# Row maxima copied into every pair of score banks by ScalarE and spread over the partitions by DMA, in place of a fourth pair of score products

## The reference

```python
x = L0_attn_queries                       # (4, 1024, 256)
xn = _layernorm(x, axis=-1)
x = x + attention(xn, Wq, Wkv, Wout, bout) + fp4_ffn(xn, w_gate, w_up, w_down)
```

## Time and profile before

| what | value |
|---|---|
| time, 3 runs | median 1957.51 us (1953.85 to 1958.97) |
| profiled execution | 1953.43 us; its span 1951.6 us |
| mean granted TensorE clock in it | 0.987 |
| busy share of the span | PE 96%, PEld 59%, DVE 76%, ACT 42%, POOL 71% |
| steady attention steps | some 475 to 1765 us of the span |

### The profile page before, as it was taken

How to read it: one execution, slowest core, us unless ns; L and a number is a source line. 1 busy time by engine, 2 the same in 40 slices (tenths; PEclk the granted TensorE clock), 3 DMA queues, 4 the chain that set the end, 5 groups by cost and what they waited for, 6 DMA issues and landing times.

```text
span 1951.6 us, 29139 instructions
## 1 busy us (share of the span) xinstructions
PE 1870.8 (96%) x10916; PEld 1151.1 (59%) x10916; DVE 1480.8 (76%) x2032; ACT 822.5 (42%) x1078; POOL 1394.7 (71%) x688
## 2 busy tenths in 40 slices
PE   6989999859999999999999999999999999999989
PEld 4768899835555555555555555555555555555589
DVE  7969999887777777777777777777777777776254
ACT  4643333214444444444444444444444444444432
POOL 4764544408888888888888888888888888889900
PEclk9989999969999999999999999999999999999999
DMA  8550311110212132122123211212322112211474
GB/s 287 227 189 30 136 36 49 47 54 20 60 53 58 53 99 62 53 64 57 54 67 95 58 53 52 63 56 57 96 64 67 54 53 58 52 50 47 144 258 171
DMA packets 151165, 161.29 MB, mean 83 GB/s; under 512 B 43248, under 2 KB 107376, under 8 KB 150768
## 3 DMA queue, kind: packets, MB, share of 16 engines
q1 hardware_dynamic: 151024, 159.43, 25.9%
HBM read 100.14 MB, written 59.24 MB: 82 GB/s over the span
## 4 chain that ended last, share of the span: by engine, by line
PE 61%; DVE 21%; issue 6%; POOL 3%; DMA 1%; ACT 0%; SPq 0%; POOLq 0%; DVEq 0%; ACTq 0%
PE banks L1004 17%; PE banks L1024 12%; PE banks L947 10%; PE banks L981 8%; PE banks L1007 6%; PE banks L1033 3%; POOL acc L1201 3%; DVE half_max L1077 3%; PE banks L1514 2%; DVE q_lo L1122 2%; DVE k_lo L1122 2%; DVE h_scales L110 2%; DVE f_y L131 2%; DVE f_amax L109 1%; DVE f_y L134 1%
## 5 line engine op out<-in xcount | busy, mean ns | idle before, releaser
L1201 POOL TENSOR_TENSOR acc<-acc,prob 128x1024 f32<-128x1024 f32 x384 | 917.4, 2389 | 131.0 <-ACT prob L1240 102.3
L1077 DVE TENSOR_REDUCE half_max<-banks 128x2 f32<-128x1024 f32 x512 | 627.5, 1227 | 298.2 <-PE banks L981 298.2
L1240 ACT ACTIVATE prob<-banks 128x1024 f32<-128x1024 f32 x512 | 512.2, 1026 | 621.5 <-PE banks L1007 621.5
L1024 PE MATMUL banks<-prob,v 128*64 128x512 f32 x2048 | 495.7, 605 | 0.0
L1024 PEld LDWEIGHTS banks<-prob,v 128*64 128x64 f32 x2048 | 124.2, 136 | 240.1 <-issue 191.2
L1201 POOL TENSOR_TENSOR acc<-prob,prob 128x1024 f32<-128x1024 f32 x64 | 153.6, 2400 | 150.3 <-ACT prob L1240 150.3
L981 PE MATMUL banks<-k_hi,q_hi 64*128 64x512 f32 x1024 | 233.4, 452 | 12.5 <-DVE half_max L1077 10.9
L947 PE MATMUL banks<-xT,wqk 128*128 128x512 f32 x768 | 217.6, 420 | 3.5 <-DVE k_lo L1122 2.1
L981 PEld LDWEIGHTS banks<-k_hi,q_hi 64*128 64x128 f32 x1024 | 97.7, 187 | 187.6 <-issue 150.5
L1007 PE MATMUL banks<-max_rows,ones_r 64*128 64x512 f32 x1024 | 203.7, 392 | 0.0
L1004 PE MATMUL banks<-q_hi,k_hi 64*128 64x512 f32 x1024 | 203.7, 393 | 0.0
(11 more groups left out here) (121 smaller groups left out, 2192.9 us busy)
## 6 DMA issues: line engine op xcount, KB each, us to landing
v_scratch<-v_out SPq DMA_DIRECT2D x32, 512.0 KB, 2.6
wqk<-wp_scratch SPq DMA_DIRECT2D x32, 512.0 KB, 3.5
v<-v_scratch SPq DMA_DIRECT2D x32, 512.0 KB, 4.8
inv_rows<-inv_scratch SPq DMA_DIRECT2D x128, 128.0 KB, 3.3
o_scratch<-o_norm SPq DMA_DIRECT2D x64, 256.0 KB, 2.0
o_in<-o_scratch SPq DMA_DIRECT2D x8, 2048.0 KB, 11.3
xn_scratch<-p_xT SPq DMA_DIRECT2D x32, 256.0 KB, 2.9
xT<-xn_scratch SPq DMA_DIRECT2D x8, 1024.0 KB, 5.8
```

The lines of the kernel that those rows point to most:

```text
L1024: ins = nc.tensor.matmul(o_ps[head * DH:(head + 1) * DH, :], v[s % 2][:, kt, at:at + DH], prob[n % SLOTS][:, head, :], start=kt == 0, stop ...
L1077: nc.vector.tensor_reduce(half_max[:, half % 2, :, t % GRP, part], guess_bank(s, i), axis=AX.X, op=ALU.max, negate=True).then_inc(half_max ...
L1201: nc.gpsimd.tensor_tensor(acc[b][:, :, :], first, prob[n % SLOTS][:, :, :], ALU.add).then_inc(added, 1)
L1240: nc.scalar.activation(prob[n % SLOTS][:, :, :], s_ps[n % 2][:, :, :], ACT.Exp).then_inc(exp_done, 1)
```

## The change

The transposition, the multiplication by the pattern, and the fourth pair of each unit's products go. In their place

- `combine` writes only the 8 columns; SP stores them to DRAM (`store_max`, new L1340, elements of 4 B), and reads all 1024 numbers (512 queries, two heads) back into each of the 128 partitions (`spread_max`, new L1349) as `max_all`,
- ScalarE copies `max_all` into the pair of score banks ahead of each unit's products (`seed`, new L1216, Copy, 128 x 1024, 512 times),
- the remaining three pairs are added on top of it, with `start=False`, and wait for `seeded`.

`seed(n+2)` stands right behind `exponent(n)` in ScalarE's order. The waits of `scores` on `exp_done` and `rows_done` become one on `seeded`; `seed(n+2)` takes over the one on `exp_done`, here on an exponential of the same engine.

```diff
@@ scores
-            if kt == 0:
-                pe.wait_ge(rows_done, 2 * s + half + 1)
-            if n >= 2:
-
-                pe.wait_ge(exp_done, n - 1)
-            elif n == 1:
-                pe.wait_ge(kept["h_high"], TILES)
+            pe.wait_ge(seeded, n + 1)
...
-                    nc.tensor.matmul(s_ps[n % 2][:, head, :], left[rows, keys], right[rows, queries], start=k == 0, stop=False)
-            for head in range(2):
-                rows = slice(head * DH, (head + 1) * DH)
-                ins = nc.tensor.matmul(s_ps[n % 2][:, head, :], ones_r[rows, :], max_rows[half][rows, :], start=False, stop=True)
+                    ins = nc.tensor.matmul(s_ps[n % 2][:, head, :], left[rows, keys], right[rows, queries], start=False, stop=k == 2,
+                                           skip_group_check=True)
             ins.then_inc(scored, 1)
@@ scalar
+        def seed(n):
+
+            s, u = divmod(n, UNITS)
+            if u % QT == 0:
+                act.wait_ge(max_in[u // QT], 16 * (s + 1))
+            if n == 0:
+                act.wait_ge(lo_done, Q0 + 1)
+            elif n == 1:
+                act.wait_ge(half_maxed, UNITS)
+            else:
+
+                act.wait_ge(exp_done, n - 1)
+            nc.scalar.activation(s_ps[n % 2][:, :, :], max_all[u // QT][:, :, :], ACT.Copy).then_inc(seeded, 1)
...
                 if scoring(s):
                     exponent(s * UNITS + 2 * r)
+                    if s * UNITS + 2 * r + 2 < STEPS * UNITS:
+                        seed(s * UNITS + 2 * r + 2)
                 if r == 0 and scoring(s + 1) and s >= 0:
                     high(act, s + 1, Q1)
                 if r in (2, 4, 6) and scoring(s + 2):
                     high(act, s + 2, CHUNK_ROUND[r - 1])
                 if scoring(s):
                     exponent(s * UNITS + 2 * r + 1)
+                    if s * UNITS + 2 * r + 3 < STEPS * UNITS:
+                        seed(s * UNITS + 2 * r + 3)
@@ sync
+        def store_max(s, half):
+
+            if s:
+
+                sp.wait_ge(max_in[half], 16 * s)
+            sp.wait_ge(max_done, 2 * s + half + 1)
+            sp.dma_start(io["max_scratch"][half].rearrange("h t p -> p h t"), max_cols[half][:, :, :],
+                         allow_slow_non_contiguous=True).then_inc(max_stored[half], 16)
+
+        def spread_max(s, half):
+
+            sp.wait_ge(max_stored[half], 16 * (s + 1))
+            if s:
+
+                sp.wait_ge(scored, (s - 1) * UNITS + (half + 1) * QT)
+            sp.dma_start(max_all[half][:, :, :].rearrange("p h c -> p (h c)"),
+                         io["max_scratch"][half].rearrange("h t p -> (h t p)").partition_broadcast(P)).then_inc(max_in[half], 16)
...
+            if scoring(s):
+                store_max(s, 1)
             if scoring(s - 1):
                 spread_inverse(2 * (s - 1))
+            if scoring(s):
+                spread_max(s, 1)
...
                 store_o(2 * (s - 1))
+            if scoring(s + 1):
+                store_max(s + 1, 0)
+                spread_max(s + 1, 0)
             if scoring(s - 1):
                 spread_inverse(2 * (s - 1) + 1)
```

More of the change, by code:

```diff
@@ L822, in misc_table @@
                 job("sum", s, 0)
[L823 to L826, removed]
     return table
@@ L850, in attention_part @@
     shuffled = [first(f"shuffled{i}", [P, GCOL], F32) for i in range(2)]
-    own = small("own", [P, GRP], F32)
     ones = small("ones", [P, DH], F32)
-    ones_r = small("ones_r", [P, P], F32R)
     half_max = small("half_max", [P, 2, 2, GRP, 2], F32)
-    max_cols = [small(f"max_cols{i}", [P, P], F32) for i in range(2)]
-    max_rows = [small(f"max_rows{i}", [P, GCOL], F32R) for i in range(2)]
+    max_cols = [small(f"max_cols{i}", [P, 2, GRP], F32) for i in range(2)]
     compact = small("compact", [P, 2, 2, GRP], F32)
@@ L868, in attention_part @@
     o_norm = [late(f"o_norm{i}", [P, GCOL], F32) for i in range(2)]
+    max_all = [late(f"max_all{i}", [P, 2, GCOL], F32) for i in range(2)]
     bout = late("bout", [P, D], F32)
@@ L883, in attention_part @@
     res_stored, wp_stored, down_done = kept["res_stored"], kept["wp_stored"], kept["down_done"]
-    guessed, half_maxed, max_done, rows_done = sem("guessed"), sem("half_maxed"), sem("max_done"), sem("rows_done")
+    guessed, half_maxed, max_done, seeded = sem("guessed"), sem("half_maxed"), sem("max_done"), sem("seeded")
+    max_stored, max_in = [sem(f"max_stored{i}") for i in range(2)], [sem(f"max_in{i}") for i in range(2)]
     scored, exp_done, pv_done, added = kept["scored"], sem("exp_done"), kept["pv_done"], kept["added"]
@@ L929, in begin @@
             pe.wait_ge(lo_done, 4 * s + k + 1)
-        elif before == "turn":
-            pe.wait_ge(rows_done, 2 * s + k + 1)
         else:
@@ L1034, in column_sums @@
             ins.then_inc(misc_done, 1)
[L1036 to L1042, removed]
+        pe.wait_ge(cleared, 1)
         for s in range(-2, STEPS + 1):
@@ L1062, in tensor @@
                     column_sums(s, 0)
[L1063 to L1066, removed]
     def vector(dve):
@@ L1082, in combine @@
             dve.wait_ge(half_maxed, s * UNITS + (half + 1) * QT)
[L1083 to L1088, removed]
             if s:
[L1091 to L1094, removed]
+                dve.wait_ge(max_stored[half], 16 * s)
+            nc.vector.tensor_reduce(max_cols[half][:, :, :], half_max[:, half, :, :, :], axis=AX.X, op=ALU.min).then_inc(max_done, 1)
         def rotate(s, chunk):
@@ L1129, in invert @@
             nc.vector.reciprocal(inv_compact[:, b, :, :], compact[:, b, :, :]).then_inc(inv_done, 1)
-        dve.wait_ge(cleared, 4)
-        dve.wait_ge(tables_in, 32)
+        dve.wait_ge(tables_in, 16)
         rotate(0, K0)
@@ L1143, in vector @@
                     maximum(s + 1, 2 * r)
-                if r == 1 and scoring(s):
-                    spread_rows(s, 1)
-                if r == 5 and scoring(s + 1):
-                    spread_rows(s + 1, 0)
                 if r == 0 and scoring(s + 1) and s >= 0:
@@ L1270, in scalar @@
                     exponent(s * UNITS + 2 * r + 1)
+                    if s * UNITS + 2 * r + 3 < STEPS * UNITS:
+                        seed(s * UNITS + 2 * r + 3)
+                elif s == -1 and r == ROUNDS - 1:
+                    seed(0)
+                    seed(1)
                 if s == STEPS - 1 and r in (2, 3, 4, 5):
@@ L1400, in clear @@
     def clear(dve):
-        nc.vector.memset(max_cols[0][:, :], 0.0).then_inc(cleared, 1)
-        nc.vector.memset(max_cols[1][:, :], 0.0).then_inc(cleared, 1)
         nc.vector.memset(ones[:, :], 1.0).then_inc(cleared, 1)
-        nc.vector.memset(ones_r[:, :].bitcast(F32), 1.0).then_inc(cleared, 1)
     def first_loads(sp):
@@ L1412, in first_loads @@
         load_x(sp, 0, 1)
-        sp.dma_start(own[:, :], io["tables"][:, P + 2 * SEQ:]).then_inc(tables_in, 16)
         load_wqk(sp, 1)
@@ L1639, in shape_constants @@
             turn[head * DH + dim, 1] = sin[:, dim // 2] if dim % 2 == 0 else -sin[:, dim // 2]
-    own = (np.arange(P)[:, None] % DH == np.arange(GRP)[None, :]).astype(np.float32)
-    return np.concatenate([np.eye(P, dtype=np.float32), turn.reshape(P, 2 * SEQ), own], 1)
+    return np.concatenate([np.eye(P, dtype=np.float32), turn.reshape(P, 2 * SEQ)], 1)
 def kernel(L0_attn_queries, L0_attn_Wq, L0_attn_Wkv, L0_attn_Wout, L0_attn_bout, L0_ffn_w_gate, L0_ffn_w_up, L0_ffn_w_down):
@@ L1675 @@
     io["sum_scratch"] = nc.dram_tensor("sum_scratch", (2, 2, GCOL), F32).ap()
+    io["max_scratch"] = nc.dram_tensor("max_scratch", (2, 2, GRP, P), F32).ap()
     io["inv_scratch"] = nc.dram_tensor("inv_scratch", (2, 2, GCOL), F32).ap()
```

## The result

| | before | after |
|---|---|---|
| time, runs shown with the result | median 1958.24 us (4 runs) | median 2013.51 us (4 runs, 2011.49 to 2015.09) |
| ratio | | 1.0286, 95% interval 1.0267 to 1.0305 |
| profiled execution | span 1951.6 us, clock 0.987 | span 2013.3 us, clock 0.968 |

The change makes the kernel 2.9% slower; 1921 us was forecast, range 1893 to 1950. The page of the changed kernel: the head, the busy shares (us, share of the span, instructions), and the chain that ended last, by engine and by line.

The account below looks back on a forecast made before the run. TensorE was taken as the bound, with VectorE's chain in round 6. Gains of 0.27 - 0.10 + 0.38 = 0.55 us a half step, 60 times, plus 1 us gave 34 us off about 1955.7: 1921 us, range 1893 to 1950.

Parts of the forecast that it names:

- So I cost the DMAs at nothing: Storing and spreading the maxima on SP's queue: hidden behind 20 us of rounds, so no time added.
- Slack 5 us: Half 1's maxima for unit 8's seed: chain of 15.3 us from the combining, needed after 20.3 us.
- the cover goes when the store's own landing passes 10.5 us: Limit for hiding the maxima's DMAs: store landing up to 10.5 us, whole chain up to 20 us.
- the chain of half 1: From the combining in round 7 to landed maxima: spread issued 10.5 us after it, landing 4.8 us later, 15.3 us.
- the bad case: Store of 1024 pieces, all time going by pieces: 9.6 us landing, chain for unit 8 19 us, still under 20.3.
- Rival 1: The 4 B store is slow and ScalarE waits for the maxima; at 14 us each, 2013 us; chance 0.10.
- the bound before: Steady attention steps: TensorE busy 1284 of 1290 us; odd rounds its own work, round 6 ending together with VectorE's chain.
- ScalarE's wait for itself: Seed behind the exponential on the same engine: starts 0.03 us after its end, taken from VectorE's pair of rows.
- round 4's working: Rounds 4 and 5 (0 and 1): TensorE waits about 0.8 us for seed b'; together 10.48 us, before 10.75, gain 0.27.
- 120 us of removed products: TensorE, two pairs a round of 0.234 us, 512 pairs in all: 120 us if nothing takes their place.
- the sums of rounds 2 and 6: They wait for VectorE's low part, now 0.10 us later behind the seed and `high`; round 5.62 us, gain -0.10.

Follow-up runs that it names:

- The runs with one half each: Changed kernel with 4 B pieces for one half alone, the other half in 128 pieces of 32 B: 1928.82 us (half 0), 1929.84 us (half 1).
- The probes: Kernel before plus single stores behind its end, each waited for, with piece number, size and spacing varied: 7.5 us for 128 x 4 B, 9.7 for 1024 x 4 B.
- 512-piece run: Changed kernel with the maxima stored in 512 pieces of 8 B in place of 1024 of 4 B: 1925.38 us, ratio 0.9845.

## Why the prediction was wrong

- **The step that failed** is "So I cost the DMAs at nothing", with "Slack 5 us" and "the cover goes when the store's own landing passes 10.5 us". I had no row for 1024 pieces. I bounded the landing by 9.6 us from the 256-piece row, and then put 5 us, which no row gave, into the sum for half 0 and 15.3 us for the chain of half 1. Where SP stands for it, the store measures 9.7 us at the least and 11.4 at the median. The bound, meant as the bad case, was the best case.
- **Rival 1 had the right mechanism and the wrong deciding point.** It gives 2013 us for a landing of 14 us. At the measured 11.4 its own sum gives 20.8 us of chain against 20.3 of cover, half a microsecond in each of 30 steps, and so some 1937 us: that the time came out at its 2013 is luck. What it lacks is SP's lap, which I never added up; I followed the chain of one half. SP waits in written order: the store of half 0 holds it 11.7 us, which makes half 1 late by 5.7. The traced chain is 5.7 + 12.5 (half 1's store and the inverse store behind it) + 1.2 + 5.3 = 24.7 us. Without the first term it is 19.0, just what my bad case had, and under the cover. The runs with one half each show it: neither store alone costs more than some 5 us.
- The rule of the Trainium skill that I set beside this rival ("DMA: Bandwidth & Descriptors", specifications: pieces under 512 B are read, changed and written) pointed the right way and I gave it too little weight, with the argument that 16 B pieces are under it too and land in 2.4 us. The probes show that under 512 B there is no one price: 1.4 us for 128 pieces of 32 B, 7.5 for 128 of 4 B. That the engine reads before it writes is seen in no run here.
- **Right:** the bound before and the rounds. With the 4 B pieces gone the kernel runs in 1924 to 1927 us against my 1921, the rounds within 0.1 us of the working, the seed at 1.028 us for 1.05, ScalarE's wait for itself at 0.03. (In round 4's working I wrote a wait of 0.85 us where its terms give 5.85 - 5.04 = 0.81; the sum does not use it.) The tip of the Trainium skill that ScalarE writes PSUM faster ("ScalarE: Activation LUTs", step by step) agrees in its direction: 1.028 against 1.050 of the earlier trace rows, 2%, though the latter's output is of another type. That of 120 us of removed products only some 31 come out has the reasons given. One is the new wait for the second seed in rounds 1 and 5: with the round ahead they take 10.45 us in the 512-piece run, where TensorE's own work would need 4.0 + 5.52, so it costs 0.9 us each time. The other is the sums of rounds 2 and 6, which wait for VectorE as before.
- **Not foreseen:** part of the loss is TensorE's clock, below; by an estimate it is less than half.

## What to carry to other kernels

- When a change puts a DMA with a wait into a queue whose order is written by hand, add up the queue's whole lap (what it stands for, in a row), not only the chain of the new transfer. A wait of 10 us that is hidden for its own consumer can make all others late, and two that are each harmless can cost 88 us together. The spare time to look for is what the queue waits for other engines (732 us here, and 59 after).
- A store of single 4 B elements whose neighbours come from different partitions is to be avoided even for a few hundred bytes; a block transposition on VectorE (0.2 us here) turns them into 128 B pieces.
- An idle engine that takes over work still has an order: what others wait for (here `high`) goes ahead of the new instruction, which gave 21 us.

## What the runs showed of the hardware

A store of 128 pieces of 4 B takes longer than one of 1024 pieces of 16 B (7.5 against 3.1 us); see the probes.

And TensorE was slower behind a long wait. After the wait of the seed at 911.57, the value products of that round take 3.18 us, against 1.94 in the round before:

```profile
908.76 1.94 PE L1009 MATMUL banks<-prob,v 128*64 128x512 f32 x8
...
916.16 3.18 PE L1009 MATMUL banks<-prob,v 128*64 128x512 f32 x8
```

The table of stages of 6 us there (busy us, instructions; after POOL the granted clock, DMA share, GB/s):

```profile
906.00:912.00 6.00, 5.12 (x26) 2.22 (x22) 4.85 (x8) 1.46 (x2) 3.23 (x3) 1.00 0.75 215
912.00:918.00 6.00, 4.31 (x20) 1.86 (x22) 2.72 (x4) 5.94 (x7) 3.91 (x3) 0.77 0.25 50
```

The granted clock is 0.77 on the mean, so TensorE ran at the lower of its two levels for a part of it, behind two waits of 1.5 and 1.0 us. In the runs without 4 B pieces TensorE waits 0.6 us at the most between 475 and 1725 us, and the clock there is 1.00. Over the span it is 0.968 against 0.985 with 512 pieces. An estimate from these two bounds its part of the 88 us: (1 - 0.968) x 2013 = 64.4 us of full clock were not granted, against (1 - 0.985) x 1923 = 28.8, so at most some 36 us are the clock, and at least some 52 the waits themselves. No run separates them further.
